# W2 of the second expert bank in one resident tile, seven result buffers in turn, and all result stores from SyncE's queue

## The chip, the cores and the metric

One core of a Trainium2 chip runs the whole program once. The metric is the device time of that core in microseconds (us). TensorE (PE) multiplies; PEld is its load of stationary operands. VectorE (DVE), ScalarE (ACT) and GpSimd (POOL) work elementwise, SyncE (SP) does nothing but issue transfers. SP, ACT and POOL each have a queue from which transfers are issued; the transfers of all of them run on the same 16 DMA engines.

## What is computed

The program is one layer over 625 nodes with 512 features in float32: a relational graph convolution and a mixing block, and then a feed-forward part with experts. Only the last part is touched:

```python
B, T, D, FF, E = (32, 1024, 512, 128, 8)
def _bank_residual(x2, Wr, br, W1, b1, W2, b2):
    logits = x2 @ Wr + br
    probs = jax.nn.softmax(logits, axis=-1)
    expert = jnp.argmax(probs, axis=-1)
    gate = jnp.take_along_axis(probs, expert[:, None], axis=-1)[:, 0]
    ...
    h = jax.nn.gelu(jnp.einsum('ecd,edf->ecf', buf, W1) + b1[:, None, :], approximate=False)
    out = jnp.einsum('ecf,efd->ecd', h, W2) + b2[:, None, :]
    y = out.reshape(e * CAP, d)[slot]
    return y * (gate * keep.astype(x2.dtype))[:, None]
shared = jax.nn.gelu(x2 @ Ws1 + bs1, approximate=False) @ Ws2 + bs2
y = shared
y = y + _bank_residual(x2, Wr_sp, br_sp, W1_sp, b1_sp, W2_sp, b2_sp)
y = y + _bank_residual(x2, Wr_fq, br_fq, W1_fq, b1_fq, W2_fq, b2_fq)
```

Each of the 625 rows goes to one of eight experts in a first bank (`sp`) and to one of eight in a second bank (`fq`). W1 of an expert is 512 x 128, its W2 128 x 512; either is 256 KB.

## The kernel before

**Blocks and tiles.** The rows are sorted by expert and cut into blocks, each of one expert. The first bank has blocks of 32 rows, four of which make a *tile* (7 tiles, `NY`, the last with three blocks); its hidden rows are already computed and only need their W2. The second bank has 12 blocks of 128 rows (`NB_FQ`). Which expert a block has is known only at run time: VectorE writes the 39 numbers into `block_ei` (L1214), and an engine that needs one loads it into a register (TENSOR_LOAD, L601 on SP, L1566 on ACT).

**A round.** The stage is a loop over rounds i = 2 to 11 (PE from L2161; SP's loop from L662; ACT's from L1584; DVE's from L1251). In round i TensorE does, in this order: `turn_rows(i+1)` turns the 128 rows of block i+1 (4 transposes, L2071, of `x_raw`); `block_first(i)` multiplies them by W1 (4 multiplies, L2081, of `w1_home`); for i - 2 < 7 `block_tile(i-2)` multiplies a tile of the first bank by the W2 of its four blocks (L2102, of `w2_home`); `block_second(i-2)` multiplies block i-2 of the second bank by its W2 (one multiply, L2090, of `w2_fq`). A float32 multiply shows as two MATMUL rows. After round 11 come the second multiplies of blocks 10 and 11, the shared expert (`shared`), and the sums of `ffn_mm`. ACT and DVE take the results out of PSUM by turns into `ybuf` (L1562, L1240); stores carry them to `y_dram` (L478). At the end POOL gathers each row's result from there, the first bank's five tiles (`gather(0)`) when the first bank's stores have landed and all rows are turned (`hT_t`), then the second bank's (`gather(1)`) when its stores have landed (L823 to L827). DVE adds them (L1266, L1276) and SP stores the output.

**Buffers.** Blocks' rows have 5 buffers (`x_raw`), W1 of the second bank 6, W2 of the second bank 6 (`w2_fq`), W2 of a tile 6 homes of which the last tile reuses home 3. Each result has a place of its own in `ybuf`.

**SP's queue** sets the order of the loads. It works strictly in order, and a wait holds all that is behind it. Once the numbers are there it issues W2 of tile 0 (4 transfers), W1 of blocks 0 to 3, W2 of tile 1, the rows of blocks 0 to 4 (`load_rows`, which waits for the scatter of the rows and for `unit_lo`), W1 of blocks 4 and 5, W2 of blocks 4 and 5, W2 of tiles 2 and 3, W2 of blocks 0 to 3, and then its loop (L662). The loop issues, for i = 5 to 11, rows of block i, W1 of block i+1, W2 of tile i-1 (waiting at tile 6 until PE is through with tile 3) and from i = 8 on W2 of a block. Each transfer is 256 KB (the last tile's three blocks make three). The stores of tiles 0 to 6 and blocks 0 to 6 go from ACT's queue one round after their result, those of blocks 7 to 11 from SP's.

## Time and profile before

| | us |
|---|---|
| median of 3 runs | 512.4 |
| lowest and highest | 512.1 and 517.22 |
| the profiled execution's own time | 514.25 |
| its span, first to last instruction | 512.4 |
| PE busy | 458.7 (90%) |
| DVE, ACT, POOL busy | 214.5, 167.5, 177.2 |
| moved by DMA | 121.37 MB, mean 237 GB/s |

The span is what the trace counts; 1.85 us of the execution's own time lie around it. The stage that is changed runs from about 440 to 490 us, and its results are gathered up to 508 us. Nothing before 400 us is touched by the change.

### The profile page before, as it was taken

Reading aid. Unit: us, or ns where it says so; the run is one execution under the profiler, and the core shown is the slowest. Engines: PE = TensorE matmul, PEld = TensorE weight load, DVE = VectorE, ACT = ScalarE, POOL = GpSimd, SP = SyncE. Lnnn points to the kernel's source line nnn. Section 1 sums busy time; section 2 is a strip of 40 time slices with the busy share of each in tenths; the row PEclk is TensorE's granted clock in tenths of the full one; section 3 lists DMA queues with packets and bytes.
Section 4 is the critical chain, followed back from the end, with each engine's and each line's share of the span. In section 5 each row is a group of like instructions: output and inputs, shape, how many; then the busy total and the mean of one; then the engine's idle time right before and its main releaser. Section 6 shows DMA issues by size and latency. Waiting matters only on the chain.

```text
span 512.4 us, 7421 instructions
## 1 busy us (share of the span) xinstructions
PE 458.7 (90%) x2602; PEld 322.1 (63%) x2602; DVE 214.5 (42%) x518; ACT 167.5 (33%) x365; POOL 177.2 (35%) x198
## 2 busy tenths in 40 slices
PE   2799799979999999898999999999999999967990
PEld 2344447758665745575577877877777787834570
DVE  4779971222352727353311012430015588512226
ACT  2799673312310021820222023340044521312320
POOL 3102100073410712296145744306026439500062
PEclk9999999989999999999999999999999999989897
DMA  5999999858999969876604541130012018999966
GB/s 120 391 424 420 424 427 363 320 221 297 383 397 422 347 201 413 350 264 201 253 1 109 178 190 57 15 92 5 0 42 63 0 49 250 349 362 335 352 190 194
DMA packets 40164, 121.37 MB, mean 237 GB/s; under 512 B 7402, under 2 KB 7463, under 8 KB 31678
## 3 DMA queue, kind: packets, MB, share of 16 engines
q1 hardware_dynamic: 34782, 113.40, 59.6%
q0 software_dynamic: 3360, 3.86, 2.9%
q10 hardware_dynamic: 1984, 3.61, 1.9%
q8 instruction: 23, 0.38, 0.3%
q14 instruction: 15, 0.12, 0.1%
HBM read 106.02 MB, written 14.82 MB: 236 GB/s over the span
## 4 chain that ended last, share of the span: by engine, by line
PE 75%; issue 7%; DMA 6%; POOL 4%; DVE 3%; ACT 3%; SPq 2%; DVEq 1%; POOLq 0%
PE ps L1607 14%; PE ps L1609 13%; PE ps L1608 13%; PE ps L1631 9%; PE ps L1966 9%; DMA ring<-in_L_gnn_basis_dram 4%; PE ps L1692 3%; POOL got L827 2%; PE ps L2081 2%; PE ps L1811 2%; PE ps L2090 1%; ACT h_tmp L1347 1%; PE ps L2102 1%; PE ps L1615 1%; DMA x_raw<-x_dram 1%
## 5 line engine op out<-in xcount | busy, mean ns | idle before, releaser
L1631 PE MATMUL ps<-ring,sel_att 128*32 128x512 f32 x512 | 66.0, 602 | 7.0 <-DMA ring<-in_L_gnn_basis_dram 3.5
L1607 PE MATMUL ps<-piece_hi,ht_hi 128*125 128x512 f32 x140 | 56.1, 401 | 0.8 <-PE ps L1609 0.6
L1609 PE MATMUL ps<-piece_hi,ht_lo 128*125 128x512 f32 x140 | 55.1, 394 | 0.0
L1608 PE MATMUL ps<-piece_lo,ht_hi 128*125 128x512 f32 x140 | 55.1, 394 | 0.0
L1086 DVE SCALAR_TENSOR_TENSOR u_lo<-ps,gates,u_hi 125x512 fp32r<-125x512 f32 x20 | 15.0, 751 | 94.1 <-ACT u_hi L1493 94.1
L753 POOL CAST piece_hi<-piece_raw 128x512 fp32r<-128x512 f32 x28 | 19.8, 708 | 93.3 <-issue 55.2
L754 POOL TENSOR_TENSOR piece_lo<-piece_raw,piece_hi 128x512 fp32r<-128x512 f32 x28 | 37.8, 1349 | 13.9 <-issue 11.8
L936 DVE TENSOR_SCALAR oh_n<-iota_n,keys 125x626 f16<-125x626 f16 x100 | 37.7, 377 | 8.2 <-PE ps L1692 6.2
L1966 PE MATMUL ps<-u_hi,cf 125*125 125x512 f32 x100 | 39.9, 399 | 1.3 <-PE ps L1609 1.3
L1966 PE MATMUL ps<-u_lo,cf 125*125 125x512 f32 x100 | 39.4, 394 | 0.0
L1607 PE MATMUL ps<-ht_hi,piece_hi 128*128 128x314 f32 x96 | 31.5, 328 | 3.5 <-POOL piece_lo L754 2.9
L1692 PE MATMUL ps<-oh_n,oh_m 125*128 125x313 f16 x200 | 30.9, 311 | 4.0 <-DVE oh_m L937 4.0
L1607 PEld LDWEIGHTS ps<-piece_hi,ht_hi 128*125 128x125 f32 x140 | 26.0, 185 | 11.1 <-DVE v L1020 2.7
L1631 PEld LDWEIGHTS ps<-ring,sel_att 128*32 128x32 f32 x512 | 11.8, 108 | 30.6 <-issue 20.6
L1491 ACT ACTIVATE cf<-counts 125x626 fp32r<-125x626 int16 x20 | 14.4, 720 | 50.4 <-PE ps L1966 50.3
L1609 PE MATMUL ps<-ht_hi,piece_lo 128*128 128x314 f32 x96 | 30.2, 314 | 0.0
L1608 PE MATMUL ps<-ht_lo,piece_hi 128*128 128x314 f32 x96 | 30.1, 314 | 0.0
L1609 PEld LDWEIGHTS ps<-piece_hi,ht_lo 128*125 128x125 f32 x140 | 25.9, 185 | 6.6
L1608 PEld LDWEIGHTS ps<-piece_lo,ht_hi 128*125 128x125 f32 x140 | 26.0, 185 | 6.0
L827 POOL DMA_INDIRECT got<-y_dram,slot_u x10 | 12.7, 1270 | 48.8 <-DMA y_dram<-ybuf 46.4
L1692 PEld LDWEIGHTS ps<-oh_n,oh_m 125*128 125x128 f16 x200 | 19.5, 102 | 12.4 <-DVE oh_m L937 4.5
L1607 PEld LDWEIGHTS ps<-ht_hi,piece_hi 128*128 128x128 f32 x96 | 18.8, 195 | 13.3 <-issue 7.8
(332 smaller groups left out, 938.9 us busy)
## 6 DMA issues: line engine op xcount, KB each, us to landing
ring<-in_L_gnn_basis_dram SPq DMA_DIRECT2D x64, 1024.0 KB, 9.2
w_home<-in_L_ffn_W_sp_dram SPq DMA_DIRECT2D x27, 256.0 KB, 5.0
rel_dram<-stag SPq DMA_DIRECT2D x16, 256.0 KB, 8.0
w_raw<-rel_dram SPq DMA_DIRECT2D x8, 512.0 KB, 6.9
y_dram<-ybuf ACTq DMA_DIRECT2D x13, 256.0 KB, 4.9
piece_raw<-in_L_mix_Wkqv_dram SPq DMA_DIRECT2D x3, 1024.0 KB, 10.3
x_dram<-stag SPq DMA_DIRECT2D x1, 3072.0 KB
w_home<-in_L_ffn_W_fq_dram SPq DMA_DIRECT2D x12, 256.0 KB, 6.3
```

The source lines that it names most:

```text
L753: own_step(pool.tensor_copy(hi, raw))
L754: last = pool.tensor_tensor(lo, raw, hi.bitcast(F32), ALU.subtract)
L827: pool.indirect_dma_start(got[b][:, t, :], None, y_dram[b], bass.IndirectOffsetOnAxis(ap=slot_u[:, t, b:b + 1], axis=0)).then_inc(got_fq[t ...
L936: dve.tensor_scalar(oh_n[:, s, h, :], iota_n[:], keys[:, 0, bass.ds(at, 1)], None, ALU.is_equal)
L1086: dve.scalar_tensor_tensor(out=u_lo[l][:, t, :], in0=ps[0:TP, u_bank(i), :], scalar=gates[:, t, r:r + 1], in1=u_hi[l][:, t, :].bitcast(F32 ...
L1491: act.activation(cf[:, t, :], counts[:, t, r * CW:(r + 1) * CW], ACT.Copy).then_inc(cf_ready, 1)
L1607: pe.matmul(target, a_hi, b_hi, start=first, stop=False, skip_group_check=skip)
L1608: pe.matmul(target, a_hi, b_lo, start=False, stop=False, skip_group_check=skip)
L1609: return pe.matmul(target, a_lo, b_hi, start=False, stop=last, skip_group_check=skip)
L1631: last = pe.matmul(ps[32 * c:32 * c + 32, rel_bank(ch), :], sel_att[:, ch // CHUNKS, g].rearrange("p r q -> p (r q)"), ring[slot][:, c * D ...
L1692: last = pe.matmul(ps[:, banks[h], 0:CB], oh_m[:, s, u, :], oh_n[:, s, u, CB * h:CB * (h + 1)], start=False, stop=False, skip_group_check= ...
L1966: last = pe.matmul(ps[0:TP, AGG[t], :], cf[:, m, t * TP:(t + 1) * TP], u[:, m, :], start=False, stop=close and m == NT - 1 and u is u_lo[l])
```

## The change

- W2 of the second bank is one tile `w2_fq` of 128 x 8 x 512 (all eight experts, 2 MB), loaded by one transfer once the second layer's relations are applied (`rel_applied` 4). The twelve loads of one expert's W2 are gone. TensorE loads the block's number into a register (the new `load_numbers` in its program) and takes the expert's part by it.
- W1 of the second bank has 8 buffers. The homes of the first bank's W2 are five, in four pieces each, elsewhere; tiles 5 and 6 reuse homes 0 and 1.
- All results of both banks go through seven buffers `ybuf` in turn, in the order in which they are made; from the eighth result on ACT or DVE waits, before it writes a buffer, until the store of what was in it has landed.
- All stores are issued by SP, directly behind the loads of its round: rows of block i+3, W1 of block i+6, the two stores of the results of round i, and in rounds 2 and 3 W2 of tiles 5 and 6. Five tiles' W2 are issued before the loop.

```diff
@@ buffers
-        ybuf = [place("ybuf0", [128, NY, D], F32, r_u + KB512), place("ybuf1", [128, NB_FQ, D], F32, r_ring)]
-        HOME = [0, 1, 2, 3, 4, 5, 3]
+        w2_fq = place("w2_fq", [128, E, D], F32, r_ring)
+        w1_home = [place(f"w1_home{i}", [128, KT, FF], F32, r_ring + 16384 + i * 2048) for i in range(W1S)]
+        ybuf = [place(f"ybuf{i}", [128, D], F32, r_u + KB512 + i * 2048) for i in range(YBUFS)]
...
+        HOME = [0, 1, 2, 3, 4, 0, 1]
@@ helpers
+        def y_buf(b, i):
+            return ORDER_OF[b, i] % YBUFS
+
+        def y_buf_free(b, i):
+
+            s = y_buf(b, i)
+            return y_out[s], Y_SEEN[s] + 16 * (ORDER_OF[b, i] // YBUFS)
...
@@ SyncE
             sp.wait_ge(rel_applied, 4)
+            sp.dma_start(w2_fq[:], W2_fq.rearrange("e f n -> f e n")).then_inc(w2_fq_in, 16)
             sp.wait_ge(slots_ready, 2)
...
+            load_tile(0)
             for i in range(4):
+                fq_of += load_numbers(NB + i, 1)
                 load_w1_fq(i)
-            expert_of[1] = load_numbers(4, 4)
-            load_w2(1)
+            load_tile(1)
             for i in range(XRAWS):
                 load_rows(i)
-            fq_of += load_numbers(NB + 4, 4)
             for i in range(4, W1S):
+                fq_of += load_numbers(NB + i, 1)
                 load_w1_fq(i)
...
-            for i in range(XRAWS, NB_FQ):
-                load_rows(i)
-                if i - XRAWS + W1S < NB_FQ:
-                    load_w1_fq(i - XRAWS + W1S)
-                if i - 1 < NY:
-                    load_w2(i - 1)
-                if i >= XRAWS + 3:
-                    load_w2_fq(i - XRAWS - 3 + W2S)
...
+            for j in range(2, 5):
+                load_tile(j)
+            for i in range(2, NB_FQ + 2):
+                if i + XRAWS - 2 < NB_FQ:
+                    load_rows(i + XRAWS - 2)
+                if i - 2 + W1S < NB_FQ:
+                    fq_of += load_numbers(NB + i - 2 + W1S, 1)
+                    load_w1_fq(i - 2 + W1S)
+                if i - 2 < NY:
+                    store_block(sp, 0, i - 2)
+                store_block(sp, 1, i - 2)
+                if i + 3 in (5, 6):
+                    load_tile(i + 3)
@@ VectorE, and ScalarE alike
                 dve.wait_ge(o_mm, ORDER_OF[b, i] + 1)
+                if ORDER_OF[b, i] >= YBUFS:
+                    dve.wait_ge(*y_buf_free(b, i))
@@ ScalarE
                 take_block(1, i - 2)
-                if 0 <= i - 3 < NY:
-                    store_block(act, 0, i - 3)
-                    store_block(act, 1, i - 3)
@@ TensorE
                 pe.wait_ge(hidden_ready, W_AT + i + 1)
-                pe.wait_ge(w2_fq_in[i % W2S], W2_FQ_SEEN[i % W2S] + 16 * (i // W2S + 1))
+                if i == 0:
+                    pe.wait_ge(w2_fq_in, W2_FQ_SEEN + 16)
...
             for i in range(2, NB_FQ):
+                fq_of += load_numbers(NB + i - 2, 1)
                 if i + 1 < NB_FQ:
                     turn_rows(i + 1)
...
+            fq_of += load_numbers(NB + NB_FQ - 2, 2)
             block_second(NB_FQ - 2)
             block_second(NB_FQ - 1)
```

TensorE's program in round 3, before (`basis_in3` says that W1 has landed, `basis_in7` that the block's W2 has, `edges_in` that the tile's has, `raw_in4` that the rows have):

```order
L2071 MATMUL ps<-ident,x_raw_220 128x128 [waits hidden_ready,raw_in4]
L2071 MATMUL ps<-ident,x_raw_220 128x128 x3
L2081 MATMUL ps<-xs_t_224,w_home_203 128x128 [waits hT_ready,basis_in3]
L2081 MATMUL ps<-xs_t_224,w_home_203 128x128 x3
L2102 MATMUL ps<-w_home_209,sorted_h 32x512 [waits hidden_ready,edges_in]
L2102 MATMUL ps<-w_home_209,sorted_h 32x512 x3
L2090 MATMUL ps<-w_fq_226,hs_232 128x512 [waits y_act,basis_in7,hidden_ready]
```

and the same round of the changed program:

```order
L2073 TENSOR_LOAD block_ei
L2083 MATMUL ps<-ident,x_raw_242 128x128 [waits hidden_ready,raw_in4]
L2083 MATMUL ps<-ident,x_raw_242 128x128 x3
L2093 MATMUL ps<-xs_t_246,w_home_204 128x128 [waits hT_ready,basis_in3]
L2093 MATMUL ps<-xs_t_246,w_home_204 128x128 x3
L2115 MATMUL ps<-w_home_0_220,sorted_h 32x512 [waits hidden_ready,edges_in]
L2115 MATMUL ps<-w_home_1_221,sorted_h 32x512
L2115 MATMUL ps<-w_home_2_222,sorted_h 32x512
L2115 MATMUL ps<-w_home_3_223,sorted_h 32x512
L2103 ISA [waits y_act,hidden_ready]
L2103 MATMUL ps<-w_fq,hs_248 128x512
```

A number load stands in front of the round, and an instruction that works out an address (ISA) in front of the last multiply; the wait for that multiply's weights is gone.

SP's queue where its loop begins, before (rows, then W1, then W2 of tile 4, then the next rows):

```order
L639 DMA x_raw_216<-x_dram 128x512 [waits hT_t]
L620 ISA [waits h_mm]
L620 DMA w_home_200<-in_L_ffn_W_fq_dram 128x512
L613 ISA [waits h_mm]
L613 DMA w_home_212<-in_L_ffn_W_sp_dram 128x512
...
L613 DMA w_home_212<-in_L_ffn_W_sp_dram 128x512
L639 DMA x_raw_217<-x_dram 128x512 [waits hT_t]
```

and there in the changed program:

```order
L648 DMA x_raw_238<-x_dram 128x512 [waits hT_t]
L617 TENSOR_LOAD block_ei
L638 ISA [waits h_mm]
L638 DMA w_home_201<-in_L_ffn_W_fq_dram 128x512
L493 DMA y_dram<-ybuf_209 128x512 [waits y_act]
L493 DMA y_dram<-ybuf_210 128x512 [waits y_dve]
L617 TENSOR_LOAD block_ei
L631 ISA [waits o_mm]
L631 DMA w_home_0_216<-in_L_ffn_W_sp_dram 128x512
...
L631 DMA w_home_3_219<-in_L_ffn_W_sp_dram 128x512
L648 DMA x_raw_239<-x_dram 128x512 [waits hT_t]
```

Between the rows of block 5 and those of block 6 stand seven transfers now, two of them stores that wait for a result; there were five.

## Rows read from the trace of the kernel before

**Rows 1.** Stretches: PE, PEld, DVE, ACT, POOL busy (instructions); PEclk, DMA share, GB/s
```profile
396.00:418.00 22.00, 21.02 (x120) 17.07 (x119) 14.08 (x41) 10.31 (x15) 5.24 (x11) 1.00 0.00 1
...
453.00:468.50 15.50, 15.26 (x89) 9.03 (x89) 3.96 (x6) 4.46 (x9) 0.00 (x0) 0.89 1.02 371
...
484.00:493.00 9.00, 9.00 (x50) 6.87 (x49) 3.01 (x5) 2.88 (x7) 5.69 (x5) 1.00 0.72 209
...
453.50:457.50 4.00, 4.00 (x18) 2.78 (x21) 0.69 (x1) 0.63 (x2) 0.00 (x0) 0.57 1.05 396
```

**Rows 2.** TensorE by time: start, us, line, what, count [idle before <-releaser]
```profile
453.24 1.71 PE L2090 MATMUL ps<-w_fq,hs 128*128 128x512 f32 x2 [4.62 <-issue]
...
459.21 0.63 PE L2071 MATMUL ps<-ident,x_raw 128*128 128x128 f32 x4
...
461.67 1.12 PE L2090 MATMUL ps<-w_fq,hs 128*128 128x512 f32 x2
462.63 0.63 PE L2071 MATMUL ps<-ident,x_raw 128*128 128x128 f32 x4
...
472.68 0.75 PE L2071 MATMUL ps<-ident,x_raw 128*128 128x128 f32 x4 [3.05 <-DMA x_raw<-x_dram]
...
477.79 0.64 PE L2071 MATMUL ps<-ident,x_raw 128*128 128x128 f32 x4
...
483.43 0.63 PE L2071 MATMUL ps<-ident,x_raw 128*128 128x128 f32 x4
...
486.54 2.74 PE L2090 MATMUL ps<-w_fq,hs 128*128 128x512 f32 x6
```

**Rows 3.** SP's queue by time: start, us to the last issue's end, line, count
```profile
447.72 1.81 SPq L629 DMA_DIRECT2D w_fq<-in_L_ffn_W_fq_dram  x4
450.93 0.33 SPq L639 DMA_DIRECT2D x_raw<-x_dram  x1
...
465.35 1.36 SPq L613 DMA_DIRECT2D w_home<-in_L_ffn_W_sp_dram  x3
```

**Rows 4.** Loads of rows (L639): us to landing, of all twelve, then of block 5's
```profile
DMA to landing us min/median/max: 4.1/5.3/8.0
...
DMA to landing us min/median/max: 4.8/4.8/4.8
```

**Rows 5.** Loads of numbers into registers on SP, ACT and TensorE: ns min/median/max
```profile
L601 SPq TENSOR_LOAD <-block_ei x10: 299/404/5335, 418.3 to 450.2; - x10
...
L1566 ACTq TENSOR_LOAD <-block_ei x9: 282/552/1105, 434.8 to 484.7; - x9
...
L1680 PEldq TENSOR_LOAD <-range_i x10: 301/304/488, 11.8 to 70.2; - x10
```

**Rows 6.** TensorE around one of its number loads, which runs between L1631 and L1685
```profile
40.40 1.07 PE L1631 MATMUL ps<-ring,sel_att 128*32 128x512 f32 x8 [0.32 <-PE ps L1631]
41.40 0.20 PE L1685 MATMUL ps<-iota_n,zeros 125*128 125x2 f16 x2
...
41.40 0.11 PEld L1685 LDWEIGHTS ps<-iota_n,zeros 125*128 125x128 f16 x2 [0.84 <-issue]
```

**Rows 7.** The end: GpSimd's gathers by time, then a piece of the chain
```profile
486.09 1.31 POOL L827 DMA_INDIRECT got<-y_dram,slot_u  x1 [43.55 <-DMA y_dram<-ybuf]
...
492.25 1.43 POOL L827 DMA_INDIRECT got<-y_dram,slot_u  x1 [0.30 <-issue]
496.49 1.21 POOL L827 DMA_INDIRECT got<-y_dram,slot_u  x1 [2.81 <-DMA y_dram<-ybuf]
...
502.84 5.45 DMA got<-y_dram,slot_u
```

**Rows 8.** Stores (L478): the last one's issue and landing, then the landing at 486.6
```profile
L478 SPq DMA_DIRECT2D y_dram<-ybuf x1: 319/319/319, 489.9 to 489.9; - x1
DMA to landing us min/median/max: 6.3/6.3/6.3
...
DMA to landing us min/median/max: 2.0/2.0/2.0
```

86 lines of the change are left out of this document (40 added, 46 removed).

## The prediction

> **What bounds the kernel now.** I read the page's 40 slices first: in the slices from about 435 to 485 us the DMA engines are nearly full, which they are nowhere else in the last fifth, and TensorE has its only two gaps there. A table of stretches puts numbers to it. From 396 to 418 us the DMA engines stand still; from 453 to 468.5 they are full (share 1.02) at 371 GB/s [rows 1], so a transfer of 256 KB (262 KB in thousands) takes its share of 262 / 371 = 0.71 us. That is the price of one transfer below, wherever the queue is full.
>
> TensorE's own timeline then says what the stage waits for [rows 2]. A normal round with a tile runs from 459.21 to 462.63, 3.42 us, without a gap. Round 2 stands still for 4.62 us in front of its last multiply, and round 7 for 3.05 us for the rows of block 8. SP's queue explains both. W2 of block 0 is issued at 447.72, because it stands behind W2 of tiles 2 and 3, though it is needed at 448.6. And the queue is held at tile 6 (which waits for tile 3's multiply) until 465.35, with the rows of block 8 behind it [rows 3]. After the first wait the granted clock is 0.57 from 453.5 to 457.5, so for most of it at 1.2 instead of 2.4 GHz [rows 1]; the first multiplies take 1.71 instead of 1.12 us, and the round after the second wait takes 472.68 to 477.79 = 5.11 us, 1.69 more than 3.42 [rows 2].
>
> Last I followed the chain that ended last. From the second multiplies of blocks 10 and 11 (end 486.54 + 2.74 = 489.28 [rows 2]) it goes through the last result's store (issued 489.9, 6.3 us to landing [rows 8]), the five gathers of the second bank from 496.49 on, the landing of the last of them (502.84 + 5.45) [rows 7] and the output. So what TensorE gains by 489 us comes off the end, as long as the stores and gathers follow.
>
> **The change, part by part.** Rounds are as in the description of the kernel.
>
> *Twelve loads of W2 go from the full stretch, one of 2 MB comes where the DMA engines idle* (396 to 418, share 0.00 [rows 1]). At 371 GB/s it takes 2,097 KB / 371 = 5.7 us from about 400, so it has landed 40 us before it is needed: cost 0. The relief, 12 x 0.71 = 8.5 us, counts only where a transfer was waited for.
>
> *Round 2* loses its wait of 4.62 us. Its last multiply then ends at 449.7, and round 3 at 449.7 + 3.42 = 453.1.
>
> *Round 4* wants the rows of block 5, and these come no earlier. Between the rows of block 4 and those of block 5 SP issued 16 transfers and seven number loads before (2 W1, 2 + 4 W2 of the second bank, 8 for tiles 2 and 3), and issues 16 and seven now (4 W1, 12 for tiles 2, 3 and 4). So they are issued at 450.9 [rows 3] and land 4.8 us later [rows 4], at 455.7. A new wait of 455.7 - 453.1 = 2.6 us takes the place of the old one.
>
> *Round 5* wants the rows of block 6. Behind those of block 5 come W1, two stores, tile 5's four and then they: 8 transfers x 0.71 = 5.7 us, landing at 461.4. SP itself needs about 0.52 us for each (three in 1.36 + 0.2 us at 465.35 [rows 3]) and 0.4 to 0.9 for each of two number loads [rows 5], some 5.2 in all, so the rows are issued at 456.1 and with the same 4.8 us would land at 460.9: the full queue decides, narrowly. TensorE would be there at 455.7 + 3.42 = 459.1: a wait of 2.3 us. *Round 6*: W1, two stores, tile 6's three, rows of block 7, 7 x 0.71 = 5.0, so 466.4, against 461.4 + 3.42 = 464.8: 1.6 us. *Round 7*: W1, two stores, rows, 4 x 0.71 = 2.8, so 469.2, against 466.4 + 3.42 = 469.8: no wait. Tile 6 now waits for tile 1, long done. Round 8 starts at 469.8 + 3.42 = 473.2, where before it starts at 477.79 [rows 2]: **4.6 us gained**. From there on each round has four transfers at most, 2.8 us of 3.42, and TensorE keeps its old pace.
>
> Its bounds: were the pace 0.66 (396 GB/s, the fastest stretch of [rows 1]), rounds 5 and 6 would start at 461.0 and 465.7 and the gain would be 5.3. Were the clock halved for one round that waits for nothing, as after both waits before, 1.7 us less: 2.9. I take no such loss, because the three waits now are 2.6, 2.3 and 1.6 where those before were 4.62 and 3.05, and because a slow round before 466 us only fills time that the rows are waited for.
>
> The Trainium skill speaks against this pace. Its page "DMA: Bandwidth & Descriptors", section "Where 436 GB/s comes from", says that transfers between HBM and SBUF are bound at about 358 GB/s for a core. The rows show 371 and 396, so the trace does not agree. By the page's figure, as an estimate, a transfer takes 0.73 us and the rows of block 7 land 0.3 us later.
>
> *TensorE loads 11 numbers and works out 12 addresses.* TensorE's number loads elsewhere take 0.30 us (at most 0.49), ACT's in this stage 0.55 (at most 1.1) [rows 5]. Around one of the former the next weights are loaded 0.84 us after the last, and yet the next multiply starts at 41.40 while the ones before it run to 41.47 [rows 6]: the sequencer runs ahead of the array, and a load is hidden if about 0.8 us of multiplies are queued. In front of each new load stands a second multiply of 1.12 us. I take 0.2 us in all. Bounds: 0; and 0.84 + (0.72 - 0.30) = 1.26 us each if nothing hides them (0.72 is about the middle of ACT's upper half), see the rivals.
>
> The skill prices this load higher: the same page, "Latency and other measured facts", gives a `tensor_load` a floor of about 600 ns. The rows show 0.30 on TensorE, half of it. By the page each would come close to what the multiply before it covers, and 11 of them unhidden would, as an estimate, be 6.6 us.
>
> *ACT loses two issues a round*, but TensorE does not wait for ACT in a normal round: 0. *SP gets them* in front of the next round's rows. The rows of block i+3 are issued in round i, once the results of round i-1 are there, and are wanted in round i+2. That is two rounds, 6.8 us, less about 1.3; 5.5 us against a median landing of 5.3 in the full stretch, which is no longer full [rows 4]. For the rows of block 11, it is 4.3, since a round without a tile takes 483.43 - 477.79 - 3.42 = 2.2 us [rows 2]. Cost 0. *Seven buffers:* a result waits for the store of the seventh before it, three and a half rounds or 12 us earlier. A store is issued within a round and lands within 6.3 us even at the end [rows 8]; cost 0. *W1's two more buffers* and the moved homes: 0, no wait for them stood anywhere.
>
> *The end.* The first bank's gather starts at 486.09 [rows 7], released by the last tile's store, which ACT issued a round late; it could have started once block 11 was turned, 483.43 + 0.63 = 484.06 [rows 2]. Now SP stores that tile at once, so relative to TensorE the gather starts up to 486.09 - 0.3 - 484.06 = 1.7 us earlier. The second bank's gathers wait for the last store, which takes 6.3 us beside those gathers, where the one at 486.6 takes 2.0 [rows 8]. With the gathers' traffic shifted I take **1.2 us**. Bounds: 0, and 4.3 (6.3 - 2.0).
>
> *Sum:* 4.6 - 0.2 + 1.2 = 5.6 us. Against the profiled execution's own time, 514.25 (span 512.4 and 1.85 around it), that is 508.65. The median of the runs, 512.4, lies 1.85 below that execution, so the forecast on it is **506.8 us**. One per cent is 5.1 us; nothing smaller can be told from no change here.
>
> **The rivals.**
>
> *A: the number load holds TensorE.* If the sequencer does not get ahead through a round with waits in it, each load costs 1.26 us. In rounds 2 to 6 it falls into waits for rows; seven loads are left: 8.8 - 5.8 = 3.0 us slower, 515.4. If all eleven count, 13.9 - 5.8 gives 520.5, slower. It decides from 0.8 us a load (the gain is gone) and 1.0 us on all eleven (1% slower). For it: the 0.84 us between weight loads. Against: the multiply above that went on without a gap [rows 6]. 0.06.
>
> *B: the rows stay the bound, or the clock falls once more.* Stores now stand in one queue with the rows; if a load takes 8.0 us as the slowest did [rows 4], a round takes (8.0 + 1.3) / 2 = 4.65 us, over four rounds 4 x 1.23 = 4.9 us, leaving 0.7: 511.7. The clock's 1.7 us alone leaves 3.9: 508.5. For it: stores must wait for results, which no load did; and three waits instead of two. Together 0.32, the likeliest about 509.
>
> *C: more comes off.* The pace of 0.66 and the full 4.3 us at the end: 5.3 + 4.3 = 9.6, so 502.8; 504 if half of it. For it: the store's 6.3 us is mostly its neighbours' traffic. Against: five gathers of 1.5 us must be issued first. 0.12.
>
> *D: nothing*, since all 12 loads were hidden. The row of 4.62 us excludes it but for what the next wait takes back, which is in the sum. 0.02. That the change does not do what it says is excluded by the instruction order.
>
> My forecast has 0.48. Its own range, from its bounds without those extremes, is 505 to 508.7. **The range for 8 in 10 is 503.2 to 512.0**: it takes in C's middle and nearly all of B, and leaves out A and C's end. **Chances:** below 507.3 lie two thirds of the forecast's case (0.32), C (0.12) and a fifth of B (0.06), 0.50; above 517.5 lies most of A, 0.05; within 1% the other 0.45.
>
> **What would show it.** TensorE's idle before L2103 in round 2 gone; a wait for rows of about 2.6 us at 453, with smaller ones at 459 and 465, none later; round 8 beginning near 473; the DMA share below 0.9 from 470 on; GpSimd's first gather near 480 and its sixth near 490.5; the number loads on TensorE at 0.3 to 0.7 us with no idle time after them. I am wrong if rows are still waited for in rounds 8 to 10, if ACT or DVE waits for a store before a result, or if the weights' loads on TensorE sit idle behind L2073.

## The result, and the profile after

The changed kernel took **510.87 us** in the median, the kernel before 515.12 us beside it on the same chip, and the ratio is 0.9941 with the interval [0.9916, 0.9966]: 3.0 us faster, between 1.7 and 4.3 us. The ratio is taken over the fast executions alone and the medians over all twenty of each, so the one is not the other two divided. Two later comparisons on other chips gave 0.9957 and 0.9934, so the three together say 2.9 us. The forecast was 5.6 us, and a time of 506.8 us. Of the 4.1 us between 506.8 and 510.87, some 1.5 us lie in the base: 0.9941 of the 512.4 us that the forecast started from is 509.4 us. The other 2.6 us are what has to be explained. The 512.4 us were the median of three executions; of the twenty run beside the changed kernel it is 515.12 us. The profiled execution of the changed kernel took 509.78 us, its span is 507.8 us.

TensorE by time, the changed kernel, against [rows 2]. L2083 turns the rows of a block (L2071 before), L2103 is the second multiply of the second bank (L2090 before). The columns are start, duration, line, what, count, and in brackets the idle time before it with what ended it:

```profile
448.30 1.13 PE L2103 MATMUL ps<-w_fq,hs 128*128 x2
449.26 0.63 PE L2083 MATMUL ps<-ident,x_raw 128*128 128x128 f32 x4
...
455.03 0.75 PE L2083 MATMUL ps<-ident,x_raw 128*128 128x128 f32 x4 [2.19 <-DMA x_raw<-x_dram]
...
460.50 1.13 PE L2083 MATMUL ps<-ident,x_raw 128*128 128x128 f32 x4 [1.78 <-DMA x_raw<-x_dram]
461.43 1.92 PE L2093 MATMUL ps<-xs_t,w_home 128*128 128x128 f32 x8
...
465.54 0.63 PE L2083 MATMUL ps<-ident,x_raw 128*128 128x128 f32 x4
...
468.96 0.63 PE L2083 MATMUL ps<-ident,x_raw 128*128 128x128 f32 x4
...
472.37 0.63 PE L2083 MATMUL ps<-ident,x_raw 128*128 128x128 f32 x4
...
481.12 2.74 PE L2103 MATMUL ps<-w_fq,hs 128*128 x6
```

The wait of 4.62 us in round 2 is gone. Two waits for rows stand in its place, 2.19 us in round 4 and 1.78 us in round 5. Round 5, from 460.50 to 465.54, takes 5.04 us instead of 3.42; most of that is L2093, which takes 1.92 us instead of 1.06. The granted clock from 460.5 to 464 is 0.51, that is 1.2 GHz (second row below). Round 8 begins at 472.37 instead of 477.79, and the last second multiply ends at 481.12 + 2.74 = 483.86 instead of 489.28: TensorE is 5.4 us ahead.

Three stretches, as in [rows 1]:

```profile
453.00:468.50 15.50, 11.69 (x65) 6.87 (x66) 3.24 (x5) 3.26 (x7) 0.00 (x0) 0.89 1.04 392
...
460.50:464.00 3.50, 3.50 (x16) 2.74 (x20) 0.00 (x0) 0.96 (x2) 0.00 (x0) 0.51 1.05 399
...
470.00:482.00 12.00, 12.00 (x74) 7.71 (x73) 3.36 (x5) 4.45 (x10) 2.11 (x2) 1.00 0.64 211
```

The DMA engines are as full from 453 to 468.5 as before (1.04 against 1.02), and from 470 on, where the twelve loads are missing, they are not (0.64).

SP's queue by time, against [rows 3]: the rows of blocks 5, 6 and 7 (L648) are issued at 449.58, 454.89 and 460.35, each behind a tile's W2 (L631), those of blocks 6 and 7 behind two stores (L493) as well:

```profile
448.16 1.37 SPq L631 DMA_DIRECT2D w_home<-in_L_ffn_W_sp_dram  x3
449.58 0.42 SPq L648 DMA_DIRECT2D x_raw<-x_dram  x1
...
450.87 1.05 SPq L493 DMA_DIRECT2D y_dram<-ybuf  x2
452.61 2.23 SPq L631 DMA_DIRECT2D w_home<-in_L_ffn_W_sp_dram  x4
454.89 0.42 SPq L648 DMA_DIRECT2D x_raw<-x_dram  x1
...
458.91 1.39 SPq L631 DMA_DIRECT2D w_home<-in_L_ffn_W_sp_dram  x3
460.35 0.42 SPq L648 DMA_DIRECT2D x_raw<-x_dram  x1
```

The chain that ended last, its end, against [rows 7]. The columns are start, duration, what; "issue" is time in which nothing was waited for that the profile shows:

```profile
484.52 5.90 DMA y_dram<-ybuf
490.42 0.02 issue
...
490.66 0.82 issue
491.48 1.21 POOL got L831
...
497.95 6.31 DMA got<-y_dram,slot_u
```

The last store takes 5.90 us to land (6.3 before, [rows 8]). From its landing at 490.42 to the sixth gather it is 1.06 us; before, that gather began at 496.49, 0.28 us after the landing (489.9 + 6.3 = 496.2). And the last gather lands 6.31 us after its issue, against 5.45 us; but the output's stores now begin almost with it, where before they began 2.5 us after it. SP's queue by time, first before, then changed (L677 and L680 store the output):

```profile
505.37 4.48 SPq L677 DMA_DIRECT2D out_dram<-x  x10
```

```profile
498.70 7.13 SPq L680 DMA_DIRECT2D out_dram<-x  x10
```

From the last gather's issue to the end of the span it is 507.8 - 497.95 = 9.9 us, before 512.4 - 502.84 = 9.6: what the gather's landing takes more, the stores behind it nearly give back. From the end of the last second multiply to the end of the span it is 507.8 - 483.86 = 23.9 us, before 512.4 - 489.28 = 23.1: the end has become longer.

The number loads on TensorE and on SP, against [rows 5]:

```profile
L2073 PEldq TENSOR_LOAD <-block_ei x11: 298/301/797, 443.5 to 479.7; - x11
...
L617 SPq TENSOR_LOAD <-block_ei x19: 274/304/1762, 418.0 to 463.1; - x19
```

### The profile page after: what moved, and what is told of

Its sections match the earlier page's. It is cut to its first block, busy times and chain, and to the rows that moved or that the text cites. A ratio compares the mean times of both kernels' runs of the same rounds, so it can differ in the third digit from the quotient of the medians.

```text
span 507.8 us, 7447 instructions
## 1 busy us (share of the span) xinstructions
PE 458.6 (90%) x2602; PEld 322.8 (64%) x2602; DVE 214.9 (42%) x518; ACT 167.6 (33%) x365; POOL 177.1 (35%) x198
## 4 chain that ended last, share of the span: by engine, by line
PE 76%; DMA 7%; issue 6%; ACT 3%; DVE 3%; SPq 2%; POOL 2%; DVEq 0%; POOLq 0%
PE ps L1612 14%; PE ps L1614 13%; PE ps L1613 13%; PE ps L1636 10%; PE ps L1971 9%; DMA ring<-in_L_gnn_basis_dram 4%; PE ps L1697 3%; PE ps L2093 2%; PE ps L1816 2%; PE ps L2103 2%; ACT h_tmp L1353 1%; DMA got<-y_dram,slot_u 1%; PE ps L1620 1%; DMA y_dram<-ybuf 1%; PE ps L2083 1%
## 5 line engine op out<-in xcount | busy, mean ns | idle before, releaser
L1971 PE MATMUL ps<-u_lo,cf 125*125 125x512 f32 x100 | 39.4, 394 | 0.0
```

Source lines behind the costliest of these rows:

```text
L1971: last = pe.matmul(ps[0:TP, AGG[t], :], cf[:, m, t * TP:(t + 1) * TP], u[:, m, :], start=False, stop=close and m == NT - 1 and u is u_lo[l])
```

## The experiments

There are sixteen runs in four groups; those of a group ran on one chip and are compared with the kernel before on it. "Profiles" below are single executions, so a stage or an end is one sample, while a ratio is over many executions. "Stage" is the time from the first turn of rows to the end of the last second multiply, "end" that from there to the end of the span, each read from the run's own profile. The first pair stands ahead of them:

| kernel | stage, us | end, us | ratio to before |
|---|---|---|---|
| before, first profile | 48.57 | 23.1 | |
| changed, first profile | 43.40 | 23.9 | 0.9941 [0.9916, 0.9966] |
| after_again | 42.94 | 24.1 | 0.9957 [0.9925, 0.9989] |
| after_control | 44.00 | 24.2 | 0.9934 [0.9901, 0.9968] |
| before_again | 46.56 | 23.0 | |
| before_look2 | 46.24 | 23.8 | |
| before_look3 | 46.69 | 23.2 | |
| number_fixed | 44.18 | 26.7 | 0.9974 [0.9942, 1.0006] |
| stores_act | 43.23 | 25.1 | 0.9897 [0.9854, 0.9940] |
| stores_act_again | 42.44 | 24.2 | 0.9939 [0.9911, 0.9968] |
| before_reordered | 44.46 | 24.7 | 0.9951 [0.9915, 0.9987] |
| waits_first | 45.19 | 24.1 | 0.9954 [0.9918, 0.9989] |
| no_first_gather | 45.26 | 20.4 | 0.9899 [0.9864, 0.9934] |
| rows_early | 39.09 | 24.1 | 0.9839 [0.9790, 0.9888] |
| best | 39.44 | 23.8 | 0.9837 [0.9796, 0.9879] |
| six_w1 | 38.60 | 24.4 | 0.9872 [0.9822, 0.9923] |
| before_rows_early | 48.48 | 23.4 | 1.0038 [1.0005, 1.0072] |
| twelve_extra | 40.22 | 29.1 | 0.9984 [0.9949, 1.0018] |

**after_again, after_control: the changed kernel once more.** No edit.

> The changed kernel once more, unchanged, as the yardstick for what is run beside it. If the stage's timing is set by the order of SP's queue, TensorE's waits for rows come back in the same two rounds (4 and 5) at 1.5 to 3 us each, the second multiplies end within 1 us of 483.9, and the time is 2 to 5 us under the kernel before. If the two waits were chance, they move to other rounds or go.

> The changed kernel as it is, a control for the others on this chip: 0.993 to 0.996 of the kernel before, 42.5 to 43.5 us from the first turn of rows to the last second multiply, waits for rows of about 2, 1.6 and 1 us in rounds 4 to 6.

510.81 us against 512.84, and 511.54 against 513.42. TensorE by time, after_again:

```profile
456.35 0.75 PE L2083 MATMUL ps<-ident,x_raw 128*128 128x128 f32 x4 [2.17 <-DMA x_raw<-x_dram]
461.56 0.75 PE L2083 MATMUL ps<-ident,x_raw 128*128 128x128 f32 x4 [1.51 <-DMA x_raw<-x_dram]
466.31 0.75 PE L2083 MATMUL ps<-ident,x_raw 128*128 128x128 f32 x4 [1.06 <-DMA x_raw<-x_dram]
```

Here no round runs at the lower clock, and so the third wait of the forecast shows, in round 6 (1.06 us). From the start of round 2 to that of round 8 this profile is only 0.5 us shorter (26.06 against 26.53 us): the round at 1.2 GHz in the first profile mostly filled this wait. In after_control it is 3.48 us in round 4 and 0.82 us in round 6, with round 5 at the lower clock between them.

**before_again, before_look2, before_look3: the kernel before once more.** No edit.

> The kernel before once more, unchanged, one look, to tell how much the profiled stage varies. From the turning of the first block to the last second multiply it took 48.6 us; if that is the order of the queue, it takes 47 to 50 again, with the long waits in rounds 2 and 7. If it was a chance, it differs by 3 us and more.

> The kernel before as it is, one more profile. Theory 1 (the half clock for the round after a wait comes in some executions and not in others, so the forecast's 4.6 us rested on one with 1.7 us of it): 46.5 us or 48.5 us from the first turn of rows to the last second multiply, according to whether the round after a wait shows the half clock. Theory 2 (that stage is always as in the first profile): 48.5 us, with 5.1 us for the round after the second wait.

> As before_look2, a further execution: 46.5 or 48.5 us by theory 1, 48.5 by theory 2.

All three show the two waits of [rows 2] (3.82 to 4.06 us instead of 4.62, and 2.77 to 3.28 about the 3.05), and in none does the round after the second wait run at the lower clock. TensorE by time, before_again:

```profile
453.53 1.29 PE L2090 MATMUL ps<-w_fq,hs 128*128 128x512 f32 x2 [4.03 <-issue]
...
455.46 1.92 PE L2081 MATMUL ps<-xs_t,w_home 128*128 128x128 f32 x8
...
473.13 0.75 PE L2071 MATMUL ps<-ident,x_raw 128*128 128x128 f32 x4 [3.28 <-DMA x_raw<-x_dram]
...
476.66 0.63 PE L2071 MATMUL ps<-ident,x_raw 128*128 128x128 f32 x4
```

The round after the second wait takes 476.66 - 473.13 = 3.53 us, where the profile that the forecast was read from had 5.11 us. From the start of round 2 to the start of round 8 these three take 29.69, 29.36 and 29.83 us, the first profile 477.79 - 446.09 = 31.70 us. The changed kernel takes 26.53, 26.06 and 27.12 us. So what TensorE gains, in the means before rounding, is 3.1 us against the three further profiles, and 5.1 us against the first. The theory that the clock's loss after the second wait comes in some executions and not in others held: it was in one of four. After the first wait the lower clock is in all four (L2081 takes 1.92 us above at 455.46, 1.91 and 1.92 in the other two, 1.73 in the first profile, instead of 1.06).

The changed kernel loses it by chance as well. waits_first and no_first_gather, described below, have the same program on TensorE and up to its last turn the same order in SyncE's queue. In both the lower clock falls on the round after the third wait, which has no wait behind it: that round takes 469.93 - 464.81 = 5.12 us in waits_first and 470.43 - 465.31 = 5.12 us in no_first_gather, 1.7 more than 3.42, and their stages are 45.19 and 45.26 us. So the loss that was in one of four profiles before is in two of five after.

**number_fixed: TensorE without its number loads.** The blocks' W2 is taken from a fixed expert instead of the block's own, so the second bank's results are other numbers.

```
-                pe.matmul(ps[:, turn_bank("o", (1, i)), :], hs[i % HSS][:], w2_fq[:, bass.ds(fq_of[i], 1), :].rearrange("p e n -> p (e n)"), start=True, stop=True).then_inc(o_mm, 1)
+                pe.matmul(ps[:, turn_bank("o", (1, i)), :], hs[i % HSS][:], w2_fq[:, i % E, :], start=True, stop=True).then_inc(o_mm, 1)
...
-                fq_of += load_numbers(NB + i - 2, 1)
...
-            fq_of += load_numbers(NB + NB_FQ - 2, 2)
```

> The changed kernel with W2 taken at fixed places (block i takes expert i modulo 8), so without the 11 number loads and 12 address steps on TensorE; the second bank's output is of the wrong experts. Theory 1, the loads are hidden behind queued multiplies: a round without waits takes 3.42 us with and without them, and the times agree within 0.5 us. Theory 2 (rival A): rounds get shorter by 0.3 to 1.3 us each, the stage by 2 us or more.

512.64 us against 512.84, not below the changed kernel's own 510.81 us of that group; by the intervals (0.3%, 1.7 us each way) rival A's gain of 2 us or more is excluded, and agreement within 0.5 us can't be told. The profile is of its longest execution (516.13 us), so its end of 26.7 us is not compared; what counts is the round. A round without a wait keeps its length to the hundredth. TensorE by time, number_fixed (in the changed kernel it is 472.37 - 468.96 = 3.41 us):

```profile
472.53 0.63 PE L2083 MATMUL ps<-ident,x_raw 128*128 128x128 f32 x4
...
475.94 0.63 PE L2083 MATMUL ps<-ident,x_raw 128*128 128x128 f32 x4
```

The loads on TensorE are hidden. Rival A is out.

**stores_act, stores_act_again: the stores back on ScalarE.** The tiles' and the first seven blocks' results are stored from ScalarE's queue again, a round later, with the seven buffers.

```
@@ SyncE, round i
-                if i - 2 < NY:
-                    store_block(sp, 0, i - 2)
-                store_block(sp, 1, i - 2)
+                if i - 2 >= NY:
+                    store_block(sp, 1, i - 2)
@@ ScalarE, round i
+                if 0 <= i - 3 < NY:
+                    store_block(act, 0, i - 3)
+                    store_block(act, 1, i - 3)
```

> The changed kernel with the stores of tiles 0 to 6 and blocks 0 to 6 from ACT's queue again, one round late as before; resident W2, seven buffers and all else as changed. Theory 1, the stores in front of the rows cost little, since the same transfers compete: waits in rounds 4 to 6 shorter by 0 to 1.5 us in sum, but the first gather 1 to 2 us later against the last multiply; the time within 1 us. Theory 2, the stores in SP's queue make the new waits: these go, 3 us and more come off.

> The changed kernel with the seven tiles' results and the first seven blocks' stored from ScalarE's queue again, one round later. Theory 1 (stores in SyncE's queue are not what costs the time; the rows are late because they stand behind W1 and W2 in the queue): the ratio to before is the control's within 0.4%. Theory 2 (the stores in SyncE's queue delay the rows): the ratio is 0.5% or more below the control's, and the waits in rounds 4 to 6 shorter by 1 us or more in sum.

508.92 us against 513.13, ratio 0.9897. That looked better than the changed kernel, which did not run on that chip, and it was run again beside it: 0.9939 against the control's 0.9934, the same. TensorE by time, stores_act:

```profile
456.08 0.75 PE L2085 MATMUL ps<-ident,x_raw 128*128 128x128 f32 x4 [2.44 <-DMA x_raw<-x_dram]
461.52 0.75 PE L2085 MATMUL ps<-ident,x_raw 128*128 128x128 f32 x4 [1.75 <-DMA x_raw<-x_dram]
466.06 0.75 PE L2085 MATMUL ps<-ident,x_raw 128*128 128x128 f32 x4 [0.85 <-DMA x_raw<-x_dram]
```

The three waits stand as in after_again: 5.0 us together against 4.7. (stores_act_again: 1.94, 1.47 and 0.84, 4.3 us; after_control beside it 3.48 and 0.82, also 4.3.) The first gather comes 3.6 us after TensorE's last turn instead of 1.6, as was expected, and the ends (25.1 and 24.2 us) are no shorter. In the medians the second group is 1.7 us better than its control (509.82 against 511.54) and in the ratios not at all, so a gain of a microsecond or two stays open; that the stores in SyncE's queue make the rows late is out.

**before_reordered: the kernel before, with only the order of its queue changed.** W2 of blocks 0 to 3 goes ahead of W2 of tiles 2 and 3.

```
+            for i in range(4):
+                load_w2_fq(i)
             for j in range(2, 4):
                 expert_of[j] = load_numbers(4 * j, 4)
                 load_w2(j)
-            for i in range(4):
-                load_w2_fq(i)
```

> The kernel before with one edit: W2 of blocks 0 to 3 is issued ahead of W2 of tiles 2 and 3. All twelve loads and the old stores stay. Theory 1, the gain of the change is mostly the order of loads: round 2 loses its wait of 4.6 us, a wait for rows of 1.5 to 3 us comes in round 4, and 1 to 4 us come off. Theory 2, it takes the twelve transfers less: what is saved in round 2 comes back in rounds 4 to 7, the time is as before within 1 us.

511.8 us against 513.13, ratio 0.9951: within the intervals (0.36%, 1.8 us each way) the same as the whole change (0.9944 in the mean of its three ratios), from lines that only moved. TensorE by time:

```profile
455.91 0.75 PE L2071 MATMUL ps<-ident,x_raw 128*128 128x128 f32 x4 [2.26 <-DMA x_raw<-x_dram]
461.07 0.75 PE L2071 MATMUL ps<-ident,x_raw 128*128 128x128 f32 x4
466.24 0.75 PE L2071 MATMUL ps<-ident,x_raw 128*128 128x128 f32 x4 [1.48 <-DMA x_raw<-x_dram]
```

The wait of round 2 is gone here too, and the rows of the later blocks are waited for in its place: 2.26 us in round 4, 1.48 in round 6 and 0.78 in round 7, 4.5 together against 4.7 in after_again. Two kernels, one with twelve transfers more, have nearly the same picture. In this order the stage goes by when the rows are issued, and the number of transfers shows only in that a wait is left in round 7.

**waits_first: GpSimd waits for the last-arriving store first.** The seven semaphores of a bank are the same, only their order is another; in front of the first bank's gathers the wait for the turned rows is moved ahead of them.

```
+                last = y_buf(b, (NY, NB_FQ)[b] - 1)
+                waits = y_stored(b)
+                waits = waits[last:last + 1] + waits[:last] + waits[last + 1:]
+                if b == 0:
+                    pool.wait_ge(hT_t, 3 * NT + NB_FQ)
-                for s, count in y_stored(b):
+                for s, count in waits:
                     pool.wait_ge(s, count)
-                if b == 0:
-                    pool.wait_ge(hT_t, 3 * NT + NB_FQ)
```

> The changed kernel, with GpSimd's waits in another order: the event that comes last (for the first gather that all rows are turned, for the second bank's gathers the store of block 11) is waited for first in the program, so that it is the wait that the gather instruction carries itself. Theory 1, the lost microsecond at the end lies in how seven waits are executed: both gathers start 0.3 us after their last event instead of 0.9 to 1.06, the end comes 0.5 to 0.8 us earlier, too little to be told by the times. Theory 2, a gather that waited long starts late whatever it waits for: still 0.8 us or more.

The chain that ended last, waits_first:

```profile
485.77 6.45 DMA y_dram<-ybuf
492.22 0.28 issue
492.51 1.21 POOL got L834
```

The sixth gather starts 0.28 us after the landing instead of 1.06 us, so the price of the waits' order is 0.8 us at this place. The end as a whole is not shorter for it, 24.1 us as in after_again: the last store is issued 0.15 us later and lands in 6.45 us instead of 6.06, and from the last gather's issue on it is 10.0 us instead of 9.8. The time shows nothing either: 511.33 us beside 510.81, ratio 0.9954 beside 0.9957, an interval of 0.35% each way (1.8 us). The stage is longer for the round at the lower clock that is told of above.

**no_first_gather: the second bank's stores without the first bank's gathers beside them.** The first bank is neither gathered nor added, so its share is missing from the result.

```
-            gather(0)
             gather(1)
...
-            dve.wait_ge(got_sp, 16 * NT)
-            for t in range(NT):
-                dve.tensor_tensor(x1[:, t, :], x1[:, t, :], got[0][:, t, :], ALU.add).then_inc(dve_own, 1)
-                n[0] += 1
```

> The changed kernel without the first bank's five gathers and without their five sums on VectorE, so the first bank's share is missing in the output. It prices the neighbours of the last store. Theory 1, the last store takes 5.9 us because it shares the DMA engines with those gathers: it lands in 2 to 3 us, the second bank's gathers start 3 to 4 us earlier, and the span falls by 3 to 5 us. Theory 2, the store is slow by itself or behind its own kind in SP's queue: 5 us or more still, and the span falls by under 1 us.

508.23 us against 512.84, where the changed kernel has 510.81: 2.6 us less than that by the medians, 3.0 by the ratios. The last two stores (L493) of no_first_gather, from issue to landing, minimum, median and maximum:

```profile
DMA to landing us min/median/max: 2.7/2.7/2.8
```

The last store lands 2.7 us after its issue instead of 5.9: the other 3.2 us are the first bank's gathers beside it. The end is 20.4 us instead of 24.1.

**rows_early: the changed kernel with the rows of each block issued earlier.** Rows of block i+5 instead of i+3 in round i, as soon as their buffer is free; tiles 2 to 4 are no longer ahead of them in one piece, and tiles 4, 5 and 6 go in rounds 2, 3 and 4.

```
-            for j in range(2, 5):
-                load_tile(j)
+            load_tile(2)
+            load_rows(5)
+            load_tile(3)
+            load_rows(6)
...
-                if i + XRAWS - 2 < NB_FQ:
-                    load_rows(i + XRAWS - 2)
...
+                if i + 5 < NB_FQ:
+                    load_rows(i + 5)
...
-                if i + 3 in (5, 6):
-                    load_tile(i + 3)
+                if i + 2 in (4, 5, 6):
+                    load_tile(i + 2)
```

> The changed kernel with another order in SP's queue: rows of block 5 before W2 of tile 3, rows of block 6 before W1 of block 6, in the loop the rows of block i+5 instead of i+3, and W2 of tiles 4, 5 and 6 in rounds 2, 3 and 4. The number of transfers is the same. Theory 1, the waits in rounds 4 to 6 are the rows' place in the queue: they go, from the first block's turning to the last second multiply it takes about 38 us instead of 43 to 45, and 4 to 6 us more come off the time. Theory 2, the DMA engines have not the throughput: the same wait turns up in front of other loads (W2 of tile 5 or 6), and under 2 us come off.

506.18 us against 513.13, ratio 0.9839 [0.9790, 0.9888]. TensorE by time, and the one idle time of this stage over 0.3 us:

```profile
449.77 0.63 PE L2086 MATMUL ps<-ident,x_raw 128*128 128x128 f32 x4
...
466.84 0.63 PE L2086 MATMUL ps<-ident,x_raw 128*128 128x128 f32 x4
...
470.03 1.06 PE L2118 MATMUL ps<-w_home,sorted_h 128*32 128x512 f32 x6 [1.66 <-DMA w_home<-in_L_ffn_W_sp_dram]
```

No round waits for rows. From 449.77 to 466.84 it is five rounds, 3.41 us each. The wait left is for W2 of tile 6. Ahead of its loads in SP's queue stands one load of a number that took 2,177 ns (L617, rows_early), more than the 1.66 us of the wait; no run takes that load away:

```profile
L617 SPq TENSOR_LOAD <-block_ei x1: 2177/2177/2177, 461.5 to 461.5; - x1
```

**before_rows_early: the rows as early in the kernel before,** with its twelve loads of W2, its six buffers for W1 and its stores on ScalarE. The order is not quite that of rows_early: tiles 4 and 5 go in rounds 2 and 3 as there, tile 6 in round 6 instead of 4.

```
+            for i in range(2):
+                load_w2_fq(i)
+            expert_of[2] = load_numbers(8, 4)
+            load_w2(2)
+            load_rows(5)
...
+            for i in range(2, NB_FQ):
+                if i + 5 < NB_FQ:
+                    load_rows(i + 5)
+                if i + 4 < NB_FQ:
+                    load_w1_fq(i + 4)
+                if i + 2 < NB_FQ:
+                    load_w2_fq(i + 2)
+                if i in (2, 3, 6):
+                    j = {2: 4, 3: 5, 6: 6}[i]
+                    expert_of[j] = load_numbers(4 * j, y_rows(j) // SB)
+                    load_w2(j)
...
```

> The kernel before with its twelve loads of W2 of the second bank and its stores on ScalarE, but the rows of each block issued as early in SyncE's queue as in rows_early, and W2 of blocks 0 and 1 ahead of tile 2's. Theory 1 (order in the queue is what the stage wants, and the twelve transfers saved are worth little once it is right): 39 to 41 us from first turn to last second multiply, 505.5 to 508 us. Theory 2 (the queue is full, so twelve transfers more at 0.7 us stay visible): waits of 3 us or more remain in rounds 2 to 7, 42.5 us or more, 509.5 us or more.

515.17 us against 513.42, ratio 1.0038: theory 1 fell, and by far. TensorE by time, and the landing of the four transfers of tile 5's W2, issued from 454.5 to 456.0:

```profile
465.91 1.94 PE L2104 MATMUL ps<-w_home,sorted_h 128*32 128x512 f32 x8 [3.00 <-DMA w_home<-in_L_ffn_W_sp_dram]
...
475.71 1.90 PE L2104 MATMUL ps<-w_home,sorted_h 128*32 128x512 f32 x6 [4.87 <-DMA w_home<-in_L_ffn_W_sp_dram]
```

```profile
DMA to landing us min/median/max: 7.1/8.2/9.8
```

The rows are never waited for, the tiles' W2 is, for 7.9 us. Transfers that were issued 7 to 8 us before their use (462.9) came 3 us too late. From 454 to 466 the DMA engines moved 398 GB/s at a share of 1.05; at that rate they move some twelve transfers in 8 us (an estimate), so about that many were under way at once. Tile 6's W2 was issued from 464.5 on, 7 us after its home was free (tile 3's multiply ends at 457.1): its place in the queue held it back, not its home.

**twelve_extra and six_w1: only the bytes.** six_w1 is rows_early with six buffers for W1, and each block's W1 a round later. twelve_extra adds twelve transfers of 256 KB to it, into two spare buffers that nobody reads; each waits for the landing of the one before last.

```
+            def load_extra(i):
+                s = 6 + i % 2
+                if i >= 2:
+                    sp.wait_ge(w1_in[s], W1_SEEN[s] + 16 * (i // 2))
+                sp.dma_start(w1_home[s][:].rearrange("p t f -> p (t f)"),
+                             W2_fq[bass.ds(fq_of[i], 1), :, :].rearrange("e f n -> f (e n)")).then_inc(w1_in[s], 16)
...
+                if i < NB_FQ:
+                    load_extra(i)
```

> rows_early with six buffers for W1 instead of eight, W1 of a block issued one round later: the control for twelve_extra. W1 still comes two rounds ahead of its use, so both theories expect rows_early's time again, 505 to 508 us, 0.982 to 0.988 of the kernel before, 39 to 40 us from first turn to last second multiply.

> The kernel of six_w1 with the twelve transfers of 256 KB put back into SyncE's queue (W2 of each block's expert, read into two spare buffers that nothing reads; W2 of the second bank stays resident). Only the traffic and the twelve issues differ from six_w1. Theory 1 (the stage is bound by bytes once the rows are early; the 9 us between before_rows_early and rows_early are the twelve transfers): waits of TensorE's of 3 us or more in sum come back in rounds 5 to 8, and the time is 3 to 9 us above that of six_w1. Theory 2 (before_rows_early was slow because tile 6's home is free late and because of the W2 homes' places, not because of the bytes): waits within 1 us of those of six_w1, and the time within 2 us of it.

505.51 us and 512.87 us, beside 513.9 for the kernel before: the twelve transfers cost 7.4 us by the medians (six and twelve executions) and 5.7 us by the ratios (0.9984 against 0.9872). But they do so at another place than theory 1 said. The stage is only 1.6 us longer (40.22 against 38.60), with no wait for rows and 1.45 instead of 0.95 us for tile 6. The end is 4.7 us longer. One stretch late in the stage, first of twelve_extra, then of six_w1 (columns as in [rows 1]), and what SP's queue waited for in twelve_extra (us in all, times, longest):

```profile
470.00:482.00 12.00, 10.39 (x51) 6.09 (x51) 2.57 (x4) 3.49 (x7) 0.00 (x0) 1.00 1.06 400
```

```profile
468.00:480.00 12.00, 11.07 (x59) 7.38 (x60) 2.77 (x4) 4.45 (x9) 2.04 (x2) 1.00 0.88 324
```

```profile
SPq L654 <- DMA w_home<-in_L_ffn_W_fq_dram: 3.4, 4, 1.3
```

With the twelve the DMA engines are still full at 482 (1.06), where the last stores and the first gathers want them. The last store of twelve_extra is issued 3.0 us after the last second multiply (485.36 against 482.33) instead of 0.9, and takes 8.4 us to land, in six_w1 5.9. About 2 us of it are this experiment's own doing, since the extra loads wait in front of the stores in one queue. So neither theory stands alone. Theory 2 was right that TensorE's waits in before_rows_early do not come from the bytes alone: with twelve transfers back and another order there are no such waits here, so the order in which the bytes stand ahead of tiles 5 and 6 has a part in them. Its own reason, tile 6's home, was not it (free at 457.1, issued from 464.5 on, waited for until 475.71). Theory 1 was right that twelve transfers are worth microseconds once the rows are early. The 9 us between before_rows_early and rows_early (on two chips; 10 us by the ratios) also hold two rounds at the lower clock (L2104 takes 1.94 and 1.90 us above; 1.06 for eight rows otherwise), each right after a wait. How they divide between bytes, order and homes was not tried further: no run gives before_rows_early the order of rows_early for tile 6.

**best: all that had shown a gain,** rows early, the last-arriving store waited for first, tile 6's W2 ahead of rows and W1 in round 4, and the first bank's gathered rows placed where no turn has to be over first.

```
-        got = [place(f"got{b}", [TP, NT, D], F32, a) for b, a in enumerate((r_raw, r_u + KB512))]
+        got = [place(f"got{b}", [TP, NT, D], F32, a) for b, a in enumerate((r_split, r_u + KB512))]
...
+                if i == 4:
+                    load_tile(6)
                 if i + 5 < NB_FQ:
                     load_rows(i + 5)
```

> The changed kernel with the rows early (as rows_early), the four loads of tile 6 ahead of the rows and W1 in their round, the last-arriving event waited for first on GpSimd, and the first bank's gathered rows put where no turn of rows has to be over first. If the waits add up as the single edits showed: no wait of TensorE's for tile 6 (1.66 us less than the 39.1 us from first turn to last second multiply of rows_early, so 37.5), the second bank's first gather 0.3 us behind the last store's landing instead of 1.06 (0.7 us less), 1 to 2.4 us less than the 506.2 us of rows_early: 504 to 505.5 us, ratio to before 0.980 to 0.984. Rival (what TensorE gains now ends in the stores and gathers): the last store lands later than 6.3 us after its issue, because the first bank's gathers stand closer to it, and the ratio stays at 0.984 or above.

504.73 us against 513.42, ratio 0.9837 [0.9796, 0.9879], the same as rows_early's 0.9839. TensorE and GpSimd by time:

```profile
467.24 1.06 PE L2121 MATMUL ps<-w_home,sorted_h 128*32 128x512 f32 x8 [1.34 <-DMA w_home<-in_L_ffn_W_sp_dram]
...
469.76 0.75 PE L2089 MATMUL ps<-ident,x_raw 128*128 128x128 f32 x4 [0.40 <-DMA x_raw<-x_dram]
```

```profile
488.79 1.21 POOL L837 DMA_INDIRECT got<-y_dram,slot_u  x1 [2.61 <-DMA y_dram<-ybuf]
```

The wait for tile 6 (1.66 us) has become one for tile 5 (1.34) and one for rows (0.40), and the stage, expected at 37.5 us, is 39.4 as in rows_early. The rows stand behind what was put ahead. Tile 5 does not: its W2 is issued 459.99 - 441.92 = 18.1 us after the stage's start where rows_early has 457.29 - 440.97 = 16.3, in one profile of each, and the cause is open. The sixth gather starts 0.3 us after the last store's landing (482.02 + 6.5 = 488.5), as it should, yet the end is only 0.3 us shorter than that of rows_early: the store's landing takes 0.2 us more and what follows the last gather's issue 0.3 us more. The kernel is 8.4 us, 1.6%, below the kernel before.

## Why the prediction was wrong

**What held.** The wait of round 2 went and the waits for rows took its place, one after the other in rounds 4, 5 and 6: forecast 2.6, 2.3 and 1.6 us, in after_again 2.17, 1.51 and 1.06 us. The rows of block 5 were forecast to be issued at 450.9 and to land at 455.7, and were issued at 449.58 and ended the wait at 455.03. Rounds 7 to 11 had no wait. The resident W2 was there at 408.2, the seven buffers and the moved stores cost nothing. A slow round before 466 us "only fills time that the rows are waited for", and mostly did. The number loads were hidden: no round got shorter without them. On both figures that the prediction took from the Trainium skill to set against the rows, the measurement decides against the figure: page "DMA: Bandwidth & Descriptors", section "Latency and other measured facts", has a floor of about 600 ns for such a load, and the eleven on TensorE took 301 ns in the median; its section "Where 436 GB/s comes from" bounds the transfers at about 358 GB/s, and the full stretch moved 392. The first gather came at 479.59 (forecast near 480), the sixth at 491.48 (near 490.5).

**The first step that failed is the stage's base:** "Round 8 starts at 469.8 + 3.42 = 473.2, where before it starts at 477.79: 4.6 us gained". The first half of it was right; in the profiled execution of the changed kernel that round started at 472.37. The second half took the one profile of before as what the kernel always does. It had 1.7 us in it, the lower clock for the round after the second wait, that none of three further profiles shows, and a first wait 0.6 to 0.8 us longer than theirs. I had seen the 1.7 us, and priced it as a bound for the changed kernel, never for the kernel before: the sum counts the loss in full before and at nothing after, where the profiles have it in one of four and in two of five. The gain that the profiles of the two kernels support is 3.1 us against those three, 3.6 against the mean of all four; with waits_first and no_first_gather taken in on the changed side it is 2.3 and 2.9. That the profiled execution lay 1.85 us above the median was no sign of the loss: that median was of three executions, and the one of the next twenty, 515.12 us, lies above the profiled one.

**The second, and the larger, is the end:** "I take 1.2 us. Bounds: 0, and 4.3". It cost 0.8 us instead (24.1 us in the mean of three profiles against 23.3 of four), outside its bounds, and 2.0 us from the forecast. Part of its reasoning held: the first gather moved nearer to TensorE's last turn, from 486.09 - 483.43 = 2.7 us to 479.59 - 478.00 = 1.6 us. But the last store gained nothing from that that can be told: 5.90, 6.06 and 6.06 us in the three profiles of the changed kernel, 6.3, 6.1 and 5.9 in three of before, since the five gathers, spaced 1.5 us, still run beside it. What stood against it: GpSimd now waits for seven semaphores, and the one that comes last is not the one it waits for first, which costs 0.8 us after the landing; the prediction priced the wait's seven buffers, not its seven waits. The other pieces of the end agree within 0.1 us in the means or cancel. Even so, an experiment doesn't confirm it: with the order of the waits turned round the end stayed at 24.1 us in waits_first, and best gained 0.3 us on rows_early. The last gather's landing, 6.3 us in all three against 5.2 to 5.45, is not a cost of its own: from its issue to the end of the span the three take 9.8 to 9.9 us, the four of before 9.6 to 10.3. The output's stores beside it, from 498.70 instead of 505.37, are the likely reason for both. no_first_gather shows that the bound of 4.3 us was real in kind, 3.2 us, but it belongs to moving the gathers out of the way, which the change does not do.

**The sum by what was measured:** stage +3.1 to 3.6, number loads 0, end -0.8, together 2.3 to 2.8 us (1.5 to 2.1 with the two further stages), against 2.9 us timed. Single profiles don't bear a tenth of a microsecond: what lies ahead of the stage ends anywhere from 439.0 to 441.7 us in the four of before. The forecast's 5.6 us came from 1.0 to 1.5 us too much in the stage and 2.0 too much in the end. That nothing under one per cent could be told from no change was wrong too: twenty executions of each gave 0.25% each way.

**The rivals.** The time fell where rival B put it (0.7 to 3.9 us gained), and part of its mechanism was right: the rows stayed the bound, and the clock fell once more in four of the five profiles with this stage, in two of them where it costs 1.7 us (waits_first, no_first_gather), in two where the next rows would have been waited for anyway, so that it costs little. That the stores in the rows' queue hold them up was not: stores_act has the same waits. B's fit is in part luck, since its sums keep the 1.2 us at the end, which did not come. Rival A is out by number_fixed. C's pace nearly came (392 GB/s against its 396), its 4.3 us at the end did not. D is out, since the time fell; but what it says of the twelve loads is nearer to what before_reordered shows than the forecast is.

**What residency was worth.** The change read as a saving of twelve transfers. before_reordered has all of them and the same time, so in this order of the queue the saving bought nothing that can be told from what a moved loop does. The pair six_w1 and twelve_extra shows that it can nevertheless be worth 6 to 7 us, of which about 2 are that experiment's own: it had to be collected by issuing the rows earlier, which the freed stretch allows and the twelve transfers would fill again.

## What to carry to other kernels

When a wait goes, count what stands in the queue ahead of the next transfer that is waited for; in a full queue the order decides first and the bytes only after it, so a change that saves transfers should be tried beside one that only reorders them. Before a gain is read off one profile, look whether the stage it comes from holds a round at the lower clock, and give the kernel before and the changed one the same chance of it. Where several semaphores release one instruction at the end of the chain, count what the wait costs behind the last event: 0.8 us here, of which 0.0 and 0.3 us came off the end in the two profiles with the order turned round.

## What the runs showed of the hardware

- A gather on GpSimd behind seven semaphore waits started 1.06 us after the last event in the changed kernel, where that event's wait came later in the program's order, and 0.28 us after it in waits_first, where its wait came first.
- The last store, of 256 KB, took 2.7 us to land without the first bank's gathers (no_first_gather), 5.9 us beside them, and 8.4 us in twelve_extra, where twelve more transfers had kept the DMA engines full until 482 us.
- A number load on SyncE took 0.30 us in the median, but 1.8 us at most in the changed kernel and 2.2 us in rows_early, ahead of the only transfers that TensorE waited for there. The same load on TensorE took 0.30 us in the median (0.80 at most) and was hidden.
- The same kernel showed the lower clock (0.51 of full speed in the second row of stretches above, 1.2 GHz) for a round in some executions and not in others. Of the fourteen profiled executions of all kernels here whose stage had a wait over 1.7 us, eleven had such a round; of the four whose longest wait was 1.66 us or less, none.
